# A state-space scan kernel: seven pairs of states per chunk summed by accumulating DMAs instead of TensorE, the residual added by DMA, and GpSimd's spreads made of tensor_scalar pieces

## What is computed

```
xc    = silu(conv(x));  delta = softplus(W_dt dt + b_dt)
state = exp(delta_t * A) * state + (delta_t * xc_t) * B_t        # 512 channels x 16 states
y_t   = sum over the 16 states n of state[:, n] * C_t[n]
y     = (y + D * xc) * silu(z)
out   = W_out y + b_out
...
result = x1 + silu(binary-weight product) * out                   # the residual x1 is layer 0's output
```

## Time and profile before

| what | value |
|---|---|
| median of 3 runs | 1458.14 us (1457.95 to 1458.37) |
| span of the profiled execution | 1456.4 us |
| median less that span | 1.7 us |
| PE, DVE, ACT, POOL busy over the span | 97%, 71%, 61%, 62% |
| first scan, last scan | 630.2 us, 1437.3 us |
| mean granted TensorE clock | 0.996 |

### The profile page before, as it was taken

The page is one execution under the profiler, slowest core; times in us unless marked ns, Lnnn a source line. Parts: engine busy times, 40 slices in busy tenths (PEclk is TensorE's granted clock), DMA queues, the critical chain, the costliest instruction groups (busy, mean ns, idle before and its releaser), DMA issues.

```text
span 1456.4 us, 24301 instructions
## 1 busy us (share of the span) xinstructions
PE 1411.8 (97%) x9148; PEld 1133.4 (78%) x9148; DVE 1029.2 (71%) x1379; ACT 890.2 (61%) x1461; POOL 909.7 (62%) x456
## 2 busy tenths in 40 slices
PE   8999999999999999979899999999999999999998
PEld 4445469999999999457777877878778778788887
DVE  8655542322322323589899899999998998998997
ACT  4211221111111111389899989999899999999993
POOL 4221211222222222159979989989989989999995
PEclk9999999999999999999999999999999999999999
DMA  9921146766767664110121120211201211211311
GB/s 311 404 78 41 57 148 222 271 242 239 267 245 257 260 239 150 41 59 31 44 73 45 41 89 33 73 59 45 88 32 43 88 44 44 74 36 39 102 42 46
DMA packets 53299, 172.70 MB, mean 119 GB/s; under 512 B 6079, under 2 KB 32319, under 8 KB 48326
## 3 DMA queue, kind: packets, MB, share of 16 engines
q1 hardware_dynamic: 46054, 150.22, 29.1%
q0 software_dynamic: 7136, 21.01, 4.3%
HBM read 141.78 MB, written 31.00 MB: 119 GB/s over the span
## 4 chain that ended last, share of the span: by engine, by line
PE 77%; DVE 10%; issue 5%; ACT 4%; POOL 2%; DMA 1%; POOLq 0%; DVEq 0%; ACTq 0%
PE bank L1498 17%; PE bank L1683 11%; PE bank L1700 11%; PE bank L1511 8%; PE bank L1443 7%; DVE hst L1334 5%; PE bank L1602 4%; PE bank L1572 3%; PE bank L1638 3%; PE bank L1610 2%; ACT dA L859 2%; PE bank L1583 2%; POOL hst L668 1%; PE bank L1473 1%; PE bank L1565 1%
## 5 line engine op out<-in xcount | busy, mean ns | idle before, releaser
L1334 DVE TENSOR_TENSOR_SCAN hst<-dA,carry,bank 128x512 f32<-128x512 f32 x512 | 632.8, 1268 | 44.8 <-PE bank L1683 43.1
L668 POOL TENSOR_TENSOR hst<-hst,c_bc 128x2048 f32<-128x2048 f32 x127 | 578.4, 4560 | 21.2 <-DVE hst L1334 6.5
L859 ACT ACTIVATE dA<-delta,negA 128x512 f32<-128x512 f32 x512 | 356.6, 713 | 0.3 <-DVE hst L1334 0.2
L1683 PEld LDWEIGHTS bank<-ident,dbuT 128*128 128x128 f32 x2048 | 245.5, 142 | 142.7 <-issue 88.3
L1683 PE MATMUL bank<-ident,dbuT 128*128 128x128 f32 x2048 | 313.1, 276 | 20.4 <-DVE hst L1334 15.3
L1700 PE MATMUL bank<-ident,hst 128*128 128x128 f32 x2016 | 291.9, 273 | 0.4 <-POOL hst L668 0.4
L848 ACT ACTIVATE dbuT<-duT,bT 128x512 f32<-128x512 f32 x382 | 271.6, 712 | 11.8 <-PE bank L1683 11.6
L1498 PEld LDWEIGHTS bank<-f_sb,w_gu 128*128 128x128 f32 x2240 | 255.5, 192 | 2.7 <-ACT f_sb L730 1.0
L1498 PE MATMUL bank<-f_sb,w_gu 128*128 128x128 f32 x2240 | 256.0, 275 | 0.7 <-ACT f_sb L730 0.7
L1700 PEld LDWEIGHTS bank<-ident,hst 128*128 128x128 f32 x2016 | 234.8, 142 | 0.6 <-POOL hst L668 0.6
L609 POOL TENSOR_TENSOR x_sb<-x_sb,neg_half 128x1 f32<-128x1 f32 x35 | 23.0, 656 | 260.7 <-DVE x_sb L1156 260.7
(11 more groups left out here) (212 smaller groups left out, 1727.7 us busy)
## 6 DMA issues: line engine op xcount, KB each, us to landing
w_gu<-in_w_gu SPq DMA_DIRECT2D x35, 2048.0 KB
c_bc<-c_rows SPq DMA_DIRECT2D x64, 512.0 KB, 3.7
sorted_x<-sg_a SPq DMA_DIRECT2D x12, 387.0 KB, 11.2
x_sb<-sorted_x SPq DMA_DIRECT2D x35, 129.0 KB
x_sb<-in_x SPq DMA_DIRECT2D x8, 512.0 KB, 7.2
w_d<-in_w_d SPq DMA_DIRECT2D x1, 4096.0 KB, 20.3
x_mix<-x_sb SPq DMA_DIRECT2D x1, 4096.0 KB, 31.4
x_mix<-rt SPq DMA_DIRECT2D x8, 512.0 KB
```

What stands on the lines that cost most here:

```text
L668: pool.tensor_tensor(h[:], h[:], c, ALU.mult).then_inc(hc_ready, 1)
L859: act.activation(dA[:, at % DA_BUFS, :], delta[q % B][:, d, :], ACT.Exp, scale=negA[:, d, n:n + 1]).then_inc(dA_ready, 1)
L1334: v.tensor_tensor_scan(h[:, d, :], dA[:, at % DA_BUFS, :], bank[4 + u % 2][:], carry1[q % B][:, n, d:d + 1], ALU.mult, ALU.add).then_inc(s ...
L1683: ins = pe.transpose(bank[4 + u % 2][:, i * P:(i + 1) * P], dbuT[(DS * q + n) % DBU_BUFS][:, i, d * P:(d + 1) * P], ident[:])
```

## The change

The kernel gets a fifth state buffer (the space comes from dropping the buffer x1 and from laying dt_sb and bc_rows into x_ld). For the pairs (0,1), (2,3) up to (12,13) POOL issues, right after its product for the odd state, a DMA that adds the even state's buffer onto the odd one's (merge; 7 in each of the chunks 0 to 6, 6 in chunk 7, 55 in all). PE then adds up only the odd state of the pair, later in the order (4(n+4)+d-1 instead of 4(n+3)+d) and behind a wait for the DMA. DVE's scan into a buffer whose state was the even one of a pair waits for that DMA; the others wait for PE's sum as before. The residual is one DMA onto g_out from DRAM, issued by POOL after state 13, in chunks 1 to 7 (7 in all), and load_x1 and DVE's last residual go. POOL's spread of a state is four tensor_scalar instructions of 512 elements (times B, times 1.0) instead of one tensor_tensor. SP's load_xn moves from c_bc's second pair to its seventh, behind waits for the users of dt_sb and bc_rows.

```diff
-STATE_BUFS = 4
+STATE_BUFS = 5
+C_BUFS = 4
-POOL_RES = (9, 11)
-SUM_AT = {(13, 0): 0, (13, 1): 3, (13, 2): 3, (13, 3): 3, (14, 0): 4, (14, 1): 4, (14, 2): 5, (14, 3): 5, (15, 0): 7,
-          (15, 1): 7, (15, 2): 8, (15, 3): 8, (0, 0): 13, (0, 1): 13, (0, 2): 14, (0, 3): 14, (1, 0): 14, (1, 1): 15,
-          (1, 2): 16, (1, 3): 17}
+POOL_RES = 13
+MERGES = {1: 0, 3: 2, 5: 4, 7: 6, 9: 8, 11: 10, 13: 12}
+LAST_MERGES = {1: 0, 3: 2, 5: 4, 7: 6, 9: 8, 11: 10}
+SUM_AT = {(13, 0): 4, (13, 1): 4, (13, 2): 5, (13, 3): 5, (14, 0): 5, (14, 1): 6, (14, 2): 6, (14, 3): 6, (15, 0): 7,
+          (15, 1): 7, (15, 2): 8, (15, 3): 8}
...
-        at = SUM_AT[n, d] if (n, d) in SUM_AT else DB * (n + 3) + d
-        SUMS_AT[at].append((int(back), n, d))
+        late = DB * (n + 4) + d - (n not in MERGES)
+        at = SUM_AT[n, d] if (n, d) in SUM_AT else late
+        if n not in MERGES.values():
+            SUMS_AT[at].append((int(back), n, d))
...
             def load_xn(c):
                 if c > 0:
                     wait_full(sp, c - 3, "XN1")
+                if c > 1:
+                    wait_full(sp, c - 2, "DL3")
+                    wait_full(sp, c - 2, "BT")
...
-                    if m == 0 and q >= 1:
-                        load_x1(q - 1)
-                    if m == 1 and q + 2 < CHUNKS:
-                        load_xn(q + 2)
+                    if m == 6 and q + 2 < CHUNKS:
+                        sp.wait_ge(c_stored, 16 * (q + 2))
+                        load_xn(q + 2)
...
-            def residual(q, h):
-                o_st = g_out[q % B][:, 2 * h:2 * h + 2, :]
-                wait_freed(pool, q + 1, f"OUT{h}")
-                pool.wait_ge(x1_in, 16 * q + 16)
-                pool.tensor_tensor(o_st, o_st, x1[:, 2 * h:2 * h + 2, :], ALU.add).then_inc(out_ready, 1)
+            def residual(q):
+                for h in range(2):
+                    wait_freed(pool, q + 1, f"OUT{h}")
+                tiles = slice(q % B * TPB + q // B * TPC, q % B * TPB + q // B * TPC + TPC)
+                pool.dma_start(g_out[q % B][:], x1_xn_t[:, tiles, 0:D], accum_op=ALU.add).then_inc(res_added, 16)
+
+            def merge(q, n):
+                g, k = DS * q + n, MERGE_NO[q, n]
+                pool.wait_ge(hc_ready, g + 1)
+                pool.dma_start(hst[g % STATE_BUFS][:], hst[(g - 1) % STATE_BUFS][:],
+                               accum_op=ALU.add).then_inc(merged[k % 2], 16)
...
-                pool.tensor_tensor(dbuT[at % DBU_BUFS][:], duT[q % B][:],
-                                   bT[q % B][:, :, n:n + 1].broadcast_to([P, TPC, DI]), ALU.mult).then_inc(dbuT_pool, 1)
+                for i in range(TPC):
+                    pool.tensor_scalar(dbuT[at % DBU_BUFS][:, i, :], duT[q % B][:, i, :], bT[q % B][:, i, n:n + 1],
+                                       1.0, ALU.mult, ALU.mult).then_inc(dbuT_pool, 1)
...
                     pool.tensor_tensor(h[:], h[:], c, ALU.mult).then_inc(hc_ready, 1)
+                    if n in merges(q):
+                        merge(q, n)
...
-                    wait_past(v, y_added, at - STATE_BUFS * DB + 1)
+                    held = divmod(DS * q + n - STATE_BUFS, DS)
+                    if held[0] >= 0 and held[1] in merges(held[0]).values():
+                        k = MERGE_NO[held[0], held[1] + 1]
+                        v.wait_ge(merged[k % 2], 16 * (k // 2 + 1))
+                    elif held[0] >= 0:
+                        v.wait_ge(y_added, ADDED[(*held, d)])
...
             def add_up(q, n, d):
 
+                if n in merges(q):
+                    k = MERGE_NO[q, n]
+                    pe.wait_ge(merged[k % 2], 16 * (k // 2 + 1))
                 pe.wait_ge(hc_ready, DS * q + n + 1)
```

More of the change, by code:

```diff
@@ L95, with merges @@
 LAST_RESULT = (45, 50)
-LAST_SUMS = {0: (14, 15, 16, 16), 1: (17, 18, 19, 19), 12: (57, 58, 59, 60), 13: (61, 62, 63, 63)}
-SUMS_AT = [[] for _ in range(UNITS)]
+LAST_SUMS = {12: (57, 58, 59, 60), 13: (61, 62, 63, 63)}
+def merges(q):
+    return MERGES if q + 1 < CHUNKS else LAST_MERGES
+SUMS_AT, SUMS_LAST = [[] for _ in range(UNITS)], [[] for _ in range(UNITS)]
 for n in (*range(DS - 3, DS), *range(DS - 3)):
@@ L101 @@
         back = n >= DS - 3
-        at = SUM_AT[n, d] if (n, d) in SUM_AT else DB * (n + 3) + d
-        SUMS_AT[at].append((int(back), n, d))
-SUMS_LAST = [[entry for entry in SUMS_AT[u] if entry[0] or entry[1] not in LAST_SUMS] for u in range(UNITS)]
+        late = DB * (n + 4) + d - (n not in MERGES)
+        at = SUM_AT[n, d] if (n, d) in SUM_AT else late
+        if n not in MERGES.values():
+            SUMS_AT[at].append((int(back), n, d))
+        if back or (n not in LAST_MERGES.values() and n not in LAST_SUMS):
+            SUMS_LAST[at].append((int(back), n, d))
 for n, at in LAST_SUMS.items():
@@ L108 @@
         SUMS_LAST[at[d]].append((0, n, d))
+MERGE_NO, ADDED = {}, {}
+for q in range(CHUNKS):
+    for n in merges(q):
+        MERGE_NO[q, n] = len(MERGE_NO)
+    for u in range(UNITS):
+        for back, n, d in SUMS_AT[u] if q + 1 < CHUNKS else SUMS_LAST[u]:
+            if q >= back:
+                ADDED[q - back, n, d] = len(ADDED) + 1
 CLAIMED = {"DT": PE_DT[0], "BC": PE_BC[0], "BT": PE_BT}
@@ L257, in build @@
         xn2T = [sb(l1, f"xn2T{b}", [P, KB, CH]) for b in range(B)]
-        dt_sb = sb(l1, "dt_sb", [P, CH])
-        bc_rows = sb(l1, "bc_rows", [P, CH])
-        x1 = sb(l1, "x1", [P, TPC, D])
+        x_ld = sb(l1, "x_ld", [P, TPC, D])
+        dt_sb, bc_rows = (x_ld[:, 2 * h:2 * h + 2, :].rearrange("p t d -> p (t d)") for h in range(2))
         c_last = sb(l1, "c_last", [P, TPC])
-        x_ld = sb(l1, "x_ld", [P, TPC, D])
         hst = [sb(l1, f"hst{i}", [P, DB, CH]) for i in range(STATE_BUFS)]
-        c_bc = sb(l1, "c_bc", [P, STATE_BUFS, CH])
+        c_bc = sb(l1, "c_bc", [P, C_BUFS, CH])
         dbuT = [sb(l1, f"dbuT{i}", [P, TPC, DI]) for i in range(DBU_BUFS)]
@@ L343, in build @@
         xn2_first = [sem(f"xn2_first{i}") for i in range(2)]
-        x1_in = sem("x1_in")
+        res_added = sem("res_added")
+        merged = [sem(f"merged{i}") for i in range(2)]
         scan_set = sem("scan_set")
@@ L657, in _ @@
                     g = DS * q + n
-                    h = hst[n % STATE_BUFS]
+                    h = hst[g % STATE_BUFS]
                     if g == CHUNKS * DS - 1:
@@ L673, in _ @@
                         spread_du(q, n + SPREAD_LEAD)
-                    if 1 <= q < CHUNKS - 1 and n in POOL_RES:
-                        residual(q - 1, POOL_RES.index(n))
+                    if q >= 1 and n == POOL_RES:
+                        residual(q - 1)
         @block.scalar
@@ L1217, in gate_y @@
             def gate_y(q, i):
-                v.wait_ge(y_added, unit(q, UNITS))
+                v.wait_ge(y_added, ADDED[q, DS - 1, DB - 1])
                 v.wait_ge(z_ready, q + 1)
@@ L1236, in dt_rows @@
                 wait_full(v, t, "DT")
-                is_freed(v.tensor_copy(dt_sb[:], place(t, "DT")[:]), t, "DT")
+                is_freed(v.tensor_copy(dt_sb, place(t, "DT")[:]), t, "DT")
             def bc(t):
@@ L1241, in bc @@
                 wait_past(v, c_stored, 16 * (t + 1))
-                is_freed(v.tensor_copy(bc_rows[:], place(t, "BC")[:]), t, "BC")
+                is_freed(v.tensor_copy(bc_rows, place(t, "BC")[:]), t, "BC")
             def turn_b(t):
@@ L1362, in _ @@
                 sum_tile(i)
-            residual(0)
             wait_freed(v, CHUNKS - 1, "G1")
             v.wait_ge(x1_last, 16)
-            tile_result(0)
-            residual(1)
-            for i in range(1, TPC):
+            for i in range(TPC):
                 tile_result(i)
@@ L1609, in dt @@
                 M = claim(t, f"DL{d}")
-                is_full(pe.matmul(M[:], w_dt[:, d * P:(d + 1) * P], dt_sb[:], start=True, stop=True), t, f"DL{d}")
+                is_full(pe.matmul(M[:], w_dt[:, d * P:(d + 1) * P], dt_sb, start=True, stop=True), t, f"DL{d}")
             def turn_b(t):
@@ L1674, in spread @@
                 if d == 0 and n in on_pool:
-                    pe.wait_ge(dbuT_pool, len(POOL_SPREADS) * q + on_pool.index(n) + 1)
+                    pe.wait_ge(dbuT_pool, TPC * (len(POOL_SPREADS) * q + on_pool.index(n) + 1))
                 elif d == 0:
@@ L1755, in turn_last @@
             def turn_last(i, d):
-                last = hst[(DS - 1) % STATE_BUFS]
+                last = hst[(DS * CHUNKS - 1) % STATE_BUFS]
                 return pe.transpose(bank[LAST_TURNED[i]][:, d * P:(d + 1) * P], last[:, d, i * P:(i + 1) * P], ident[:])
```

30 lines of the change are left out of this document (12 added, 18 removed).

## The result

The changed kernel takes 1485.72 us (median of 4 runs, 1484.43 to 1487.24) against 1458.26 us before: a ratio of 1.0186, 95% interval 1.0174 to 1.0198. It is 27 us slower; 1446 us, 12 us faster, was predicted. The profiled execution's span is 1483.0 us, 26.6 above that of before. In the experiments, two executions lay far above the others of their kernel (1967 us in the small merges, 2882 us in the later pairs) and are left out of every figure here.

A forecast was written before the change was run, and what follows sets the result against it. PE was taken to bound most of a chunk, POOL the last one. POOL's work, -40 spreads, -15 residual, +68 issues, plus 11 us of waits gave 793 against 804.8 us: -12, so 1446 us, range 1422 to 1488.

The forecast's parts named there:

- next in line: Middle chunk: DVE stands behind PE, so a chunk can't go under about 97 us, 6 us less than before.
- The rival with cheap issues: POOL's DMA issues cost 0.5 to 0.7 us, DVE sets a middle chunk at 97 us: 1416 us; chance 0.12.
- The issues: POOL issuing 55 merges and 7 residuals: 1.1 us each with the wait for its own product, +68 us.
- the deduction for the indices: POOL's indirect DMA rows, 1.26 us, also read 128 indices; a plain DMA doesn't, so 1.1 us with its wait.
- The spreads: POOL's 32 spreads become 128 pieces of 0.58 us from start to start: 74 instead of 114 us, -40 us.
- The cast's row: POOL's cast of 512 elements with one input, 0.61 us, taken as the nearest row for a spread's piece.
- POOL's waits: POOL between first carry and last product: 11 of 35.9 us of waits stay; 3.0 us early in each chunk go.
- The landing: A merge's data arriving before DVE reuses the buffer: taken as 9 us, hidden, since up to 14 us fits.
- The rival that came true: POOL's queue of products becomes the bound and costs more than PE gives back: 1465 to 1489 us; chance 0.32.
- point of decision: Cost of one DMA issue on POOL at which gains and costs cancel: 1.3 us.
- The late landing as its own rival: A merge's addition takes 20 us, making 123 us a chunk, some 1600 us in all; chance 0.06.

The follow-up runs named there:

- small merges: Changed kernel with each merge adding only 128 of a partition's 2048 elements, most of the pair sum left out: 1488.6 us.
- later pairs: Changed kernel with merges only for the pairs (6,7), (10,11), (12,13), in the last chunk the first two: 1457.6 us.
- free pairs: Changed kernel with no merge issued, PE adding up only the odd states of the pairs, even ones missing from the result: 1444.2 us.
- The run with both exits shortened: Changed kernel with merges of only 128 of 2048 elements and POOL's product of delta moved ahead of the state's product: 1465.5 us.

## Why the prediction was wrong
**What bounded the kernel before.** That PE was the bound over most of a chunk holds. That DVE, at 97 us a chunk, was next in line does not: the free pairs stop at 101.1 us, with ScalarE in their chain. The busy times of the earlier trace rows were read as if the longest one gave the next floor. But a chunk has stretches with different bounds, and ScalarE's 22 us in one piece can't be seen in its 96.3 us. The rival with cheap issues (1416 us) rested on this; even with issues at nothing it is 1444.

**The issues: mis-sized.** A merge took 1.26 us on POOL instead of 1.1, the residual 1.32, together 55 x 1.26 + 7 x 1.32 = 78.5 us instead of 68: 10 us. The indirect rows (1.26 from start to start) were the right measure as they stood, and the deduction for the indices was not. The Trainium skill, "DMA: Bandwidth & Descriptors", Latency and other measured facts, puts the emission at about 1 us; the instruction itself took 0.89 here, so the trace agrees with it. The wait for the product came out at 0.30, not 0.15.

**The spreads: mis-sized.** A piece took 0.665 us from start to start instead of 0.58: 85 us for all, not 74, so 29 us saved and not 40. The cast's row was too cheap a model; why, no run shows. The Trainium skill, "GPSIMD Engine Reference", Performance versus the Vector engine, has 769 ns for 512 elements in a tight loop, unrolled four times (not the one-instruction loop that the prediction calls it); here it is 665 from start to start and 695 for one record in the run with the spreads alone, between its figure and the cast.

With these two sizes put right and nothing else, the sum would have been 1446 + 10 + 11 = 1467 us: already slower. So these two terms turned the sign; the third, the waits, made most of the rest.

**POOL's waits: the mechanism that failed.** The sum kept 11 of 35.9 us of waits, since POOL "then has a backlog" at the start of a chunk. It kept 26 us (829.4 less 768.9 - 29 - 15 + 78.5 = 803.4 us of work; read as waits for DVE and PE they are 24.4), and the 3.0 us early in a chunk that were to go are there as before. A backlog that lasts over the chunk's border needs the next chunk to start while POOL is behind, and two things forbid it: DVE needs the buffers of the late merges, and PE needs the last product of delta. The landing was checked against the average pace of four states (14 us were allowed, 9.1 came), which is right for the middle of a chunk; but when POOL is late at its end, the landing is added to its lateness, 7 times in the chain. The run with both exits shortened has 5.5 us of waits where the prediction wanted 11, and comes to 1465.5 us with all issues in place, close to the 1467 of the sum with the two sizes put right.

In us of the span: work of the issues +10, of the spreads +11, waits +15, a start 2 us later (637.05 against 635.09) and 1 of rounding: 39, from 1444 to 1483.

**The rival that came true** is the second, POOL costing more than PE gives back, at 0.32. Its point of decision, 1.3 us for each issue, was worked out with most waits gone and the pieces at 0.58: 79.7 / 62. With 0.665 it falls to (79.7 - 11) / 62 = 1.11, and with 26 us of waits to 0.87 us: the measured 1.26 lies well above. Both mistakes moved the point to the same side, and it was near the taken value from the start. That 1485.7 us still lies in the stated 1422 to 1488 is luck: its upper end was drawn for issues of 1.8 us with most of the waits gone. The late landing as its own rival (20 us) didn't come; 9.1 us was right.

## What to carry to other kernels
Where several engines are busy over 90% of a period, as here, the second longest busy time is no floor: ask for each stretch of the period which engine is back to back in it, and run once with the relief for free (the work simply left out) before paying for it. Work given to an engine with 4% of idle time needs to fit where that engine is idle; a backlog absorbs a wait only if nobody needs that engine's last result of the period, or the landing of its last DMA, before the next one starts. An accumulating DMA issued by GpSimd cost its queue 1.26 us here with the wait for its own product, so that seven of them in a chunk outweighed 112 transposes of PE (1465.5 us with both exits short, 1460.6 without merges).

## What was not expected of the hardware
An accumulating DMA of 1 MB from SBUF onto SBUF held GpSimd for 0.87 to 0.99 us and landed in 7.8 to 10.6 us; with a sixteenth of the data it held it just as long and landed in 4.0 us. The residual, 512 KB in rows of 1 KB from DRAM, landed in 11.5 us in the median. It is issued right behind the merge of state 13; without merges it landed in 7.9 us, behind a small one in 6.9, so much of the 11.5 goes with the 1 MB ahead of it.

TensorE's granted clock fell where PE had waited, here for a landing. Windows of the kernel after, at the start of the last chunk (columns as above):

```profile
1370.00:1375.00 5.00, 2.54 (x16) 1.62 (x16) 3.40 (x3) 5.00 (x9) 5.00 (x2) 1.00 0.99 174
1375.00:1380.00 5.00, 4.00 (x19) 4.00 (x20) 3.59 (x3) 5.00 (x9) 5.00 (x2) 0.51 0.55 123
```

PE in order of time there:

```profile
1373.46 0.66 PE L1703 MATMUL bank<-ident,dbuT 128*128 128x128 f32 x4 [0.45 <-DVE hst L1363]
1376.00 1.97 PE L1723 MATMUL bank<-ident,hst 128*128 128x128 f32 x8 [1.89 <-DMA hst<-hst]
```

In the five microseconds from 1370 us, PE was busy half of the time; in the next five the granted clock is 0.51 (the lower level, 1.2 GHz, of the two), and eight transposes take 1.97 us instead of the 0.87 of the earlier trace rows. Over the whole run the mean granted clock is 0.987 against 0.996. An engine relieved of work that then waits can so lose part of its relief again. In the changed kernel's chain this is small: the pieces of PE between 1376.0 and 1383.5 us take 7.5 us, where the same ones take 4.4 at full clock, and one more place costs 0.9, some 4 of the 27 us (an estimate). In the small merges it is more, some 11 us.
